# A two-layer graph kernel: the neighbours' attention product as one 96-row f16 product, and three weight loads from another queue

## What is computed

```
x  : 4096 x 256 f32      adj : 4096 x 4096 int32, a mask of 0 and 1      neigh : 4096 x 256 f32
layer 0:  agg = mask @ x / max(degree, 1)
          x1  = layernorm(x + relu([x@W_self + b_self, agg@W_nb + b_nb] @ W_comb + b_comb))
layer 1:  neib_att = tanh(neigh @ Wn1 + bn1) @ Wn2 + bn2        (4096 x 32)
          value    = neigh @ Wv + bv                            (4096 x 128)
          x_att    = tanh(x1 @ Wx1 + bx1) @ Wx2 + bx2           (4096 x 32)
          ws  = softmax(where(adj > 0, leaky_relu(x_att @ neib_att.T), -9e15))
          out = layernorm(x1 + [x1@Wfx + bfx, ws @ value])
```

## Time and profile before

| | |
|---|---|
| median of 3 runs | 729.9 us (729.87 to 730.22) |
| the profiled execution's own time | 730.62 us |
| its span, first to last instruction | 728.8 us |
| PE busy | 689.6 us, 95% |
| PEld busy | 592.1 us, 81% |
| DVE busy | 621.7 us, 85% |
| ACT busy | 573.5 us, 79% |
| POOL busy | 129.9 us, 18% |
| mean granted TensorE clock | 0.994 of full |

### The profile page before, as it was taken

How to read it: one execution, slowest core, us unless ns; L and a number is a source line. 1 busy time by engine, 2 the same in 40 slices (tenths; PEclk the granted TensorE clock), 3 DMA queues, 4 the chain that set the end, 5 groups by cost and what they waited for, 6 DMA issues and landing times.

```text
span 728.8 us, 19763 instructions
## 1 busy us (share of the span) xinstructions
PE 689.6 (95%) x7344; PEld 592.1 (81%) x7344; DVE 621.7 (85%) x1535; ACT 573.5 (79%) x920; POOL 129.9 (18%) x242
## 2 busy tenths in 40 slices
PE   5989998999999999999999999999999999998775
PEld 4646676888888888888888888888888888886554
DVE  4887668999999999999999999999999999987874
ACT  2455248888888888888888888888888888889884
POOL 0010111222211222221111222211122221111101
PEclk9989999999999999999999999999999999999999
DMA  8967999999999999999999999999999999841111
GB/s 266 370 150 165 228 269 236 195 203 223 196 202 206 223 208 202 216 224 213 220 212 208 208 203 219 188 221 205 206 200 217 212 220 217 167 81 33 39 42 44
DMA packets 260145, 141.39 MB, mean 194 GB/s; under 512 B 225361, under 2 KB 243665, under 8 KB 260049
## 3 DMA queue, kind: packets, MB, share of 16 engines
q1 hardware_dynamic: 259604, 140.10, 88.7%
q10 hardware_dynamic: 444, 0.02, 0.0%
HBM read 81.35 MB, written 4.19 MB: 117 GB/s over the span
## 4 chain that ended last, share of the span: by engine, by line
PE 86%; ACT 5%; DVE 4%; issue 3%; POOL 1%; DMA 1%; SPq 0%; POOLq 0%; ACTq 0%
PE ps_v L1137 22%; PE ps_agg L1092 15%; PE ps_agg L1095 14%; PE ps_t L1116 10%; PE ps_s L1107 7%; PE ps_agg L1156 3%; PE ps_agg L1159 3%; PE ps_s L1006 2%; PE ps_v L1014 2%; PE ps_x L1176 1%; PE ps_x L1179 1%; ACT score L913 1%; PE ps_t L997 1%; PE ps_x L1023 1%; DMA neigh_sb<-in_L_gnn_neigh_dram 1%
## 5 line engine op out<-in xcount | busy, mean ns | idle before, releaser
L1092 PE MATMUL ps_agg<-x,mask_t 128*128 128x257 f16 x1024 | 243.4, 274 | 0.2 <-DMA mask_t<-mask 0.2
L1095 PE MATMUL ps_agg<-x,mask_t 128*128 128x256 f16 x1024 | 237.4, 273 | 0.3 <-DVE x L533 0.3
L907 ACT ACTIVATE score<-ps_s,sc 128x512 f32<-128x512 f32 x256 | 178.7, 698 | 63.1 <-PE ps_s L1107 57.6
L692 DVE CUSTOM_DVE_ANT_0 score<-score,mask 128x512 f32<-128x512 f32 x256 | 175.9, 687 | 16.7 <-ACT score L907 14.3
L1137 PEld LDWEIGHTS ps_v<-v,late 128*128 128x128 f16 x2304 | 143.9, 97 | 41.7 <-DVE late L756 16.9
L1137 PE MATMUL ps_v<-v,late 128*128 128x129 f16 (+1 forms) x2304 | 162.6, 219 | 11.6 <-DVE late L773 6.0
L913 ACT ACTIVATE score<-score,exp_bias,sc 128x1024 f32<-128x1024 f32 x128 | 159.4, 1246 | 3.2 <-DVE exp_bias L701 3.2
L756 DVE TENSOR_TENSOR late<-ps_t,late 128x512 f16<-128x512 f32 x192 | 130.7, 681 | 33.2 <-ACT late L920 31.4
L920 ACT CAST late<-ps_t 128x512 f16<-128x512 f32 x192 | 114.8, 598 | 20.4 <-PE ps_t L1116 20.4
L1116 PE MATMUL ps_t<-ident,score 128*128 128x128 f32 x768 | 116.8, 275 | 5.3 <-ACT score L913 5.1
L1095 PEld LDWEIGHTS ps_agg<-x,mask_t 128*128 128x128 fp8e4 x1024 | 100.3, 98 | 15.5 <-issue 5.2
(11 more groups left out here) (133 smaller groups left out, 805.4 us busy)
## 6 DMA issues: line engine op xcount, KB each, us to landing
adj_sb<-in_adj_dram SPq DMA_DIRECT2D x128, 512.0 KB, 5.3
neigh_sb<-in_L_gnn_neigh_dram SPq DMA_DIRECT2D x8, 512.0 KB, 8.0
score<-in_x_dram SPq DMA_DIRECT2D x8, 512.0 KB, 8.5
x_in<-in_x_dram SPq DMA_DIRECT2D x32, 128.0 KB, 2.7
out_dram<-out_sb SPq DMA_DIRECT2D x32, 128.0 KB, 3.3
mask_t<-mask SPq DMA_TRANSPOSE x128, 4.8
neigh_sb<-neigh_sb SPq DMA_TRANSPOSE x64, 3.7
mask<-in_L_gnn_W_comb_dram SPq DMA_DIRECT2D x1, 512.0 KB, 9.2
```

The source lines that it names most:

```text
L692: dve.tensor_tensor_reduce(score[:, b % 2, part], score[:, b % 2, part], mask[:, b % MASK_BUFS, part], 1.0, -3.0e38, ALU.subtract, ALU.max ...
L907: act.activation(score[:, b % 2, k * GW:(k + 1) * GW], ps_s[k % 2][:, :], ACT.Prelu, alpha=SLOPE, scale=score_scale).then_inc(leaky_made, 1)
L1092: mm = pe.matmul(agg[:, 0:D + 1], mask_t8[:, c, 0, :], x16[:, c, X_HI:X_ONE + 1], start=(c == 0), stop=(c == NC - 1), skip_group_check=True)
L1095: mm = pe.matmul(agg[:, 0:D], mask_t8[:, c, 0, :], x16[:, c, X_LO:X_LO + D], start=False, stop=False, skip_group_check=True)
```

## The change

Three things are changed together.

1. The attention product. Wn1 is laid three times side by side (ACT makes the two copies), so the hidden product gives 96 rows. ACT takes the tanh of these twice, into an f32 tile h32 and an f16 tile h16. DVE's new `h_low` replaces rows 64 to 95 of h16 by h32 - h16. Wn2 becomes wn2_16, an f16 tile whose middle 32 rows hold the low half. One f16 product of 96 rows then gives high times high, high times low and low times high in one sum. h32 and h16 lie in the tile late, where res was alone before.
2. Places in the order. In the slots, `neigh_attention` moves from PE's `first_part` to the end of the slot, `h_low` takes DVE's place in that slot, and `n_high` and `n_low` move one slot later. Before the slots, `h_low` is put between the scans.
3. NEIGH_WEIGHTS are issued from ACT's queue ahead of ATT_WEIGHTS. bn1 and Wn2 are now loaded to four groups of 32 partitions.

```
-            for dst, src in NEIGH_WEIGHTS:
-                sp.dma_start(dst, src).then_inc(neigh_w_in, 16)
 ...
+            def h_low(turn):
+                dve.wait_ge(h_tanh, 2 * turn + 2)
+                part = slice(2 * H, H3)
+                dve.tensor_tensor(h16[part, :], h32[part, :], h16[part, :], ALU.subtract).then_inc(h_split, 1)
 ...
             for i in range(3, NT):
                 scan_neigh(i)
+                if i == 5:
+                    h_low(0)
 ...
             n_low(0)
             v_low(0)
+            h_low(1)
             v_low(1)
 ...
             for i in range(5, NT):
                 scan_x(i)
+                if i == 5:
+                    h_low(2)
 ...
             n_low(2)
+            h_low(3)
             dve.wait_ge(x_top_reduced, 1)
 ...
                 if (t := turn_due(s, 0)) is not None:
                     v_low(t)
+                if (t := turn_due(s - 1, 2)) is not None:
+                    n_low(t)
                 if (t := turn_due(s, 2)) is not None:
-                    n_low(t)
+                    h_low(t)
 ...
         @block.scalar
         def _(act):
+            for dst, src in NEIGH_WEIGHTS:
+                act.dma_start(dst, src).then_inc(neigh_w_in, 16)
             for dst, src in ATT_WEIGHTS:
                 act.dma_start(dst, src).then_inc(att_in, 16)
 ...
-                act.activation(h_t, ps_h[0:H, :], ACT.Tanh, bias=bn1_sb[:, 0:1]).then_inc(h_tanh, 1)
+                for out in (h32, h16):
+                    act.activation(out, ps_h[0:H3, :], ACT.Tanh, bias=bn1_sb[0:H3, 0:1]).then_inc(h_tanh, 1)
 ...
             act.wait_ge(neigh_w_in, 16 * len(NEIGH_WEIGHTS))
+            for k in range(1, 3):
+                act.copy(wn1_sb[:, :, k * H:(k + 1) * H], wn1_sb[:, :, 0:H]).then_inc(wn1_copied, 1)
 ...
-                if (t := turn_due(s, 2)) is not None:
+                if (t := turn_due(s - 1, 2)) is not None:
                     n_high(t)
 ...
-                    mm = pe.matmul(ps_h[0:H, :], wn1_sb[:, dc, :], turned(turn, dc), start=(dc == 0),
+                    mm = pe.matmul(ps_h[0:H3, :], wn1_sb[:, dc, :], turned(turn, dc), start=(dc == 0),
                                    stop=(dc == DC - 1))
 ...
             def neigh_attention(turn):
-                pe.wait_ge(h_tanh, turn + 1)
+                pe.wait_ge(h_split, turn + 1)
 ...
-                pe.matmul(ps_x[0:H3, :], wn2_sb[:, :], h_t, start=True, stop=True).then_inc(natt_done, 1)
+                pe.matmul(ps_x[0:H3, :], wn2_16[:, :], h16, start=True, stop=True).then_inc(natt_done, 1)
 ...
-                if (t := turn_due(s, 2)) is not None:
-                    neigh_attention(t)
                 if s == Z_BIAS_SLOT:
                     combine_biases()
 ...
                         weigh_values(d[0], BY_PE + 2 * w + d[1])
+                if (t := turn_due(s, 2)) is not None:
+                    neigh_attention(t)
```

More of the change, by code:

```diff
@@ L261, in gnn_kernel @@
         bounds_scaled = sem("bounds_scaled")
-        att_copied = sem("att_copied")
+        att_split = sem("att_split")
+        wn1_copied = sem("wn1_copied")
+        h_split = sem("h_split")
         v_scaled = sem("v_scaled")
@@ L1011, in neigh_hidden @@
             def neigh_hidden(turn):
-                at_least(pe, h_tanh, turn)
+                at_least(pe, h_tanh, 2 * turn)
+                if turn == 0:
+                    pe.wait_ge(wn1_copied, 2)
                 for dc in range(DC):
-                    mm = pe.matmul(ps_h[0:H, :], wn1_sb[:, dc, :], turned(turn, dc), start=(dc == 0),
+                    mm = pe.matmul(ps_h[0:H3, :], wn1_sb[:, dc, :], turned(turn, dc), start=(dc == 0),
                                    stop=(dc == DC - 1))
@@ L1018, in neigh_attention @@
             def neigh_attention(turn):
-                pe.wait_ge(h_tanh, turn + 1)
+                pe.wait_ge(h_split, turn + 1)
                 at_least(pe, natt_lo, turn)
                 if turn == 0:
-                    pe.wait_ge(att_copied, 2)
-                pe.matmul(ps_x[0:H3, :], wn2_sb[:, :], h_t, start=True, stop=True).then_inc(natt_done, 1)
+                    pe.wait_ge(att_split, 1)
+                pe.matmul(ps_x[0:H3, :], wn2_16[:, :], h16, start=True, stop=True).then_inc(natt_done, 1)
             def combine_weights():
```

39 lines of the change are left out of this document (22 added, 17 removed).

## The result

| | before | after |
|---|---|---|
| median, runs taken side by side | 729.88 us (729.43 to 731.44, 6 runs) | 741.16 us (738.61 to 742.64, 6 runs) |
| ratio, 95% interval | | 1.0147 [1.0135, 1.0158] |
| the profiled execution, its span | 730.62, 728.8 us | 740.34, 738.5 us |
| start of block 0's `combine` | 82.15 us | 91.60 us |

The change makes the kernel 11.3 us slower. Slower was forecast, but by 4.1 us, and 741.2 lies outside the range of 730.8 to 738.0. Three executions far out of line, of 1186 and 1432 us (both of experiment 4) and 1819 us (one of before, beside experiments 1 to 4), are left out of every ratio.

A forecast was written before the change was run, and what follows sets the result against it. PE was taken to bound the kernel, so first-stage shifts reach the end. Terms: -1.2 - 0.1 + 0 + 2.05 + 1.58 - 0.8 = +1.5, plus 2.6 for the clock, +4.1: 734.0 us, range 730.8 to 738.0.

The forecast's parts named there:

- The loads: At the start: rows of neigh asked for 1.54 us earlier, ACT's issues covered, all that follows shifts by -1.2 us.
- Turns 0 to 3: Before the first aggregate: f16 product savings against second tanh and h_low sum to -0.1 us, bounds -0.8 and +0.6.
- Turn 4: In slots with combine_biases between: saving and a short wait cancel, 0, from -0.8 to +0.9 us.
- Turn 5: PE waits 2.15 us for x_low(5) and 1.0 us for h_low(5); next transposes +2.05 us.
- Turn 6: h_low(6) stands behind m_low(1) and a mask on DVE; PE waits 2.4 us, values(7) +1.58 us.
- Turn 7: n_high(7) and n_low(7) no longer stand before mean_low; combine at 81.35 for 82.15, -0.8 us.
- The wider hidden product: 96 weight columns for 32, longer loads hidden under the f32 passes: 0; uncovered, 1.5 us.
- The clock: One more stretch of PE at the lower clock in 61 to 82 us, +2.6 us, between 1.7 and 3.4.
- the prediction's own sign: The prediction is wrong if, among other signs, the granted clock stays at 1.00 from 61 to 82 us.
- Two falls more: Rival: PE idles again near 46 us, clock low into the aggregates; +6.7, 736.6 us; chance 0.16.
- Waits come, clock holds: Rival: the waits of turns 5 and 6 come without a clock fall; +1.5, 731.4 us; chance 0.24.
- Faster: Rival: DVE delivers in time, PE finds h_low set on arrival; 727.8 us, or 722.3 with every saving; chance 0.12.

The follow-up runs named there:

- experiment 4: The kernel before, queues as they were, with only bn1 and Wn2 loaded to four groups of 32 partitions; 730.72 us, 0.9999.
- experiments 1 to 4: Four follow-up runs; the third, not named elsewhere, is the changed kernel with bn1's load on a semaphore of its own: 742.54 us, 1.0169.
- experiment 1: The changed kernel with the three NEIGH_WEIGHTS loads back on SP, ahead of the rows of neigh; 736.16 us, 1.0075.
- experiment 12: The kernel before with both the three loads moved to ACT's queue and the wider forms of bn1 and Wn2; 735.68 us, 1.0069.
- experiment 11: The kernel before with only the DVE order of experiment 9; 729.83 us, 0.9987.
- experiment 7: The changed kernel with SP waiting for all seven small loads before issuing the rows of neigh; one execution, 740.01 us.
- 2: The kernel before with only the three loads moved, in their old forms, to ACT's queue ahead of its four; 731.45 us, 1.0018.
- experiment 6: Experiment 1 with 104 small f16 products, results unused, placed where PE waits; 734.16 us, 1.0050.
- experiment 8: The changed kernel with ATT_WEIGHTS issued from SP ahead of the rows, NEIGH_WEIGHTS staying on ACT's queue; 735.64 us, 1.0079.
- 5: Experiment 1 with the attention product of turns 4 to 6, n_high and n_low one slot later; 729.08 us, 0.9991.
- experiment 9: Run 5 with DVE's order before the slots changed: x scale chain ahead of n_low(2) and h_low(3), first mask ahead of v_low(3); 728.24 us, 0.9970.
- experiment 10: Experiment 9 with 45 products of 256 columns that nothing reads, in PE's idle time; 732.72 us, 1.0032.

## Why the prediction missed

**The failing step is "The loads"**: -1.2 us, with bounds of 0 and 1.54. It counted what SP saves and what ACT spends in issuing, and let the weights "travel beside" the rows. In fact the rows were asked for 1.55 us earlier (0.72 for 2.27) and came 2.1 us earlier, but bn1 gates DVE's first scan, which started at 12.62 where 6.4 was forecast. Up to the first group, loads and turns 0 to 3 together were forecast at -1.3 and measured +5.30; experiment 1, which has turns 0 to 3 without the move, has +0.2 there. So the loads cost 5.1 us in that profile (5.30 - 0.2), 5.0 in the medians (741.16 - 736.16), and 5.0 to 5.6 in experiment 12. The bounds were wrong in kind: I let the weights cost no more than SP saved, when no row of before showed a small load issued beside the bulk ones and needed at once. How late such a load is stands in experiment 11, whose start is that of before: the last of ATT_WEIGHTS, issued at 3.01, was waited for till 12.31.

```profile
12.31 0.19 DVE L551 TENSOR_REDUCE sc<-wx_sb 128x1 f32<-128x32 f32 x1 [1.82 <-DMA bx_sb<-in_L_gnn_bx_dram]
```

The same step had ACT free at 5.5 us, by issues of 0.46 to 1.13 us. That sum was right for a queue with nothing beside it (5.18 in experiment 7), and 3.5 us short beside the rows (9.02).

Which property does it: not the queue with nothing beside it (7), not the forms on the old queues (4), hardly the queue with the old forms (2); queue, forms and rows in flight together (12). In the unlike cases ACT's queue carries 1036 packets (2) and 1204 (12, after). How the wider forms turn 7.08 into 12.26 us for bn1 is not shown and stays open; no run here shows on which of the 16 DMA engines a small load's pieces lay.

The Trainium skill, DMA: Bandwidth & Descriptors, section Issuing engines are not separate DMA queues, says that issuing from several engines saves only sequencer time, as all share the same 16 DMA engines. The trace agrees: SP's 1.5 us were saved, and the weights met the rows. The same page, section Rules for kernel authors, says that a DMA whose outermost dimension is a leading broadcast of c copies is kept to at most c of the engines; bn1 and Wn2 have that form now, c = 4, and it would fit, but that was not tried by itself. (bn2, Wx2 and bx2 had that form already.)

**Turns 0 to 3**, -0.1: +0.2 in experiment 1, within the bounds, but partly by luck. The first mask was issued 0.42 us earlier than before (44.70 for 45.12), and its DMA took 0.63 us longer (3.86 for 3.23), which the prediction did not have. Experiment 6, with the same order up to there, issued it at 43.92, so one profile tells this term to some 0.8 us. h_low takes 0.68 us (0.69 forecast), the f16 product 0.22 of the chain (0.22). **Turn 4**, 0: -0.13 in experiment 6, where no fall covers it. Right. **Turn 5**, +2.05: measured +2.09 (8.93 - 6.84). **Turn 6**, +1.58: +1.35. **Turn 7**, -0.8: -0.83. The wider hidden product, 0: the terms around it leave no room for 1.5. Turns 4 to 7 were forecast at +2.83 and measured +2.49 in experiment 6; with turns 0 to 3 it is +2.7 and +2.68, and that close an agreement is luck, by what was said of the first mask.

**The clock**, one more fall, +2.6 in 61 to 82 us: by the prediction's own sign this failed in the profile of the changed kernel, where the clock stayed at 1.00 from 61 to 82 us. One more fall is there, at 53.9 to 57.3, behind the wait for the first mask, which is nearer to what the rival *Two falls more* described. That waits in the first stage cost clock is right, but the place is not fixed: experiment 1's profile has falls at 48.3 and 79.0, experiment 8's at 63.6 and 77.3. The size was too large: a fall cost 1.7 us in the changed kernel (1.54 and turn 4's 0.13), 1.5 and 1.4 in experiment 1, all of them at or below the lower bound of 1.7. The 3.4 of before counted a longer stretch. Waits of equal length (2.29 us) were followed by a fall in one kernel and not in the other, so the size of one wait does not decide it.

**The account** of the changed kernel's profile, at `combine`: loads 5.1, turns 0 to 3 +0.2, the fall 1.7, turns 4 to 7 +2.5, together 9.45. The medians lie 11.3 us apart, the profiled executions 9.7. The rest is not assigned. Its likeliest place is the clock, but that is argued: four of the six executions have a mean clock of 0.988 to 0.990 and a median time near 742, the profiled one 0.994 and 740.34, and a fall near the end went with 1.3 us behind `combine` in experiment 1's profile. With the loads at their measured size the forecast would have been near 740; that it comes so close owes something to one fall priced as nearly two.

**The rivals.** *Waits come, clock holds* would give 731.4 (its own bounds add up to 729.6 to 734.1, not 730 to 733). Experiment 1's fastest run, 732.20, is near it, with a mean clock of 0.994 for 0.988 to 0.990 in the other five, but it has no profile. *Two falls more, or a late rise* came nearest in number (736.6): its place, the first aggregates behind an idle time near 46 us, is where the fall was, but there was one fall and not two, and what brought the time up to it and past it were the loads. *Faster* fell: PE did not find h_low set in slots 5 and 8. It can be had, by moving the product and not DVE's work (5, 9).

## What to carry to other kernels

Small loads that something needs at once should be issued and under way before the bulk ones, whatever queue they are on; issuing time saved on one queue is not arrival time, so bound a moved load by when its consumer would stop for it. When a shorter instruction puts a helper on another engine into the path, move the consumer back in order until the helper is done: here that turned +5.7 us (experiment 1) into no difference (5), and with one more reordering (9) into a gain of 1.8 us, though the share of that last step is not shown. And before filling idle time to keep the clock, see what the slow stretch covers: where PE would only have waited behind it, as in experiment 9, it cost little.

## What the runs showed of the hardware that was not expected

- Small loads beside bulk rows: bn1 (128 x 4 B) came 10.4 us after its issue began (1.83 to 12.28) and the last weight 12.6 us (6.11 to 18.73); with no rows in flight all were there by 7.62, the last within 3.0 us. The issuing instruction itself grew from 0.54 to 1.82 and 2.88 us.
- The effect is steep in the form of the loads: bn1 and Wn2 as four copies (128 pieces each for 32) moved bn1 from 7.08 to 12.26 us and the last weight from 15.63 to 18.74.
- Keeping PE busy held the clock at full (experiment 6), and the same means moved the fall to a worse place (experiment 10). In both, the first mask's transposing DMA took 4.6 to 4.9 us, for 3.2 to 3.9 in the others.
- PE's clock also falls near the end, in some executions: to 0.50 from 690.0 to 693.4 us in experiment 1's profile and from 682.8 to 686.2 in experiment 9's, not in before's or the changed kernel's.
